# Attention steps that mix side slots, scores and products with v, in place of turns of two steps

## What is computed

```python
x = x + 0.5 * ffn(layernorm(x));  x = x + attention(layernorm(x));  x = x + 0.5 * ffn(layernorm(x))

def ffn(x):            # weights are +1 or -1: 512 -> 1024 -> 1024 -> 256
    h = concatenate([x, -x]);  h = relu(s0 * (h @ k0)) * 2;  h = relu(s1 * (h @ k1)) * 2;  return s2 * (h @ k2)

def attention(x):      # per batch and head, 2048 queries by 2048 keys
    scores = softmax(q @ k.T / 4);  return concat_heads(scores @ v) @ wo.T + bo
```

## Time and profile before

| | us |
|---|---|
| median of 3 runs | 1490.13 |
| lowest and highest run | 1490.06, 1495.2 |
| the profiled execution | 1485.83 |
| its span, first to last instruction | 1481.8 |
| what lies around the span | 4.0 |
| PE busy | 1467.2 |
| ACT busy | 1149.8 |
| DVE busy | 594.7 |

### The profile page before, as it was taken

One profiled execution on the slowest core, in us unless ns is written; L12 is line 12 of the kernel. 1 busy time (PEld: TensorE's weight loads), 2 busy tenths in 40 slices (PEclk: granted clock), 3 DMA queues, 4 the chain that ended last, 5 costly groups with the idle time before them and its releaser, 6 DMA issues.

```text
span 1481.8 us, 69894 instructions
## 1 busy us (share of the span) xinstructions
PE 1467.2 (99%) x32431; PEld 754.9 (51%) x32431; DVE 594.7 (40%) x1330; ACT 1149.8 (78%) x1240; POOL 59.8 (4%) x65
## 2 busy tenths in 40 slices
PE   9999999999999999999999999999999999999999
PEld 4555455544455445545454554564555455445454
DVE  7546755621432253334332332332242342333461
ACT  3221221799999999999999999999899999999821
POOL 2010111001000100010100000000000000000000
PEclk9999999999999999999999999999999999999999
DMA  4121324313221341223222221322212312313010
GB/s 137 49 86 36 92 72 107 95 43 96 74 58 43 102 100 47 72 87 101 90 53 74 81 60 58 89 59 61 84 47 69 86 43 71 87 49 64 25 43 17
DMA packets 113359, 103.93 MB, mean 70 GB/s; under 512 B 58919, under 2 KB 98599, under 8 KB 113063
## 3 DMA queue, kind: packets, MB, share of 16 engines
q1 hardware_dynamic: 112230, 98.61, 25.1%
q10 hardware_dynamic: 832, 0.79, 0.2%
HBM read 61.87 MB, written 25.43 MB: 59 GB/s over the span
## 4 chain that ended last, share of the span: by engine, by line
PE 98%; DVE 1%; DMA 1%; issue 0%; SPq 0%; ACT 0%
PE psum L875 31%; PE psum L916 31%; PE psum L896 14%; PE psum L769 12%; PE psum L781 3%; PE psum L757 3%; PE psum L788 2%; PE psum L801 1%; DMA den_t<-den_rows 0%; DVE den_t L1135 0%; DMA x_sb<-in_x 0%; PE psum L794 0%; DVE stats L1059 0%; DVE xn L1001 0%; SPq L1273 0%
## 5 line engine op out<-in xcount | busy, mean ns | idle before, releaser
L971 ACT ACTIVATE prob<-psum 128x1024 f32<-128x1024 f32 x1024 | 1032.0, 1026 | 64.1 <-PE psum L896 25.6
L916 PE MATMUL psum<-prob,v_sb 64*17 64x512 f32 x8192 | 552.7, 589 | 0.2 <-issue 0.2
L896 PE MATMUL psum<-q_st,k_st 64*32 64x512 f16 (+1 forms) x7736 | 481.3, 376 | 3.2 <-issue 3.1
L944 ACT ACTIVATE h_hi<-psum 128x512 f16<-128x512 f32 x183 | 108.3, 597 | 211.4 <-PE psum L769 165.8
L896 PEld LDWEIGHTS psum<-q_st,k_st 64*32 64x32 f16 (+1 forms) x7736 | 154.1, 92 | 203.2 <-ACT prob L971 77.5
L916 PEld LDWEIGHTS psum<-prob,v_sb 64*17 64x17 f32 x8192 | 152.7, 93 | 147.4 <-issue 80.0
L1011 DVE SCALAR_TENSOR_TENSOR h_lo<-psum,h_hi 128x512 f16<-128x512 f32 x256 | 168.3, 687 | 82.8 <-ACT h_hi L944 80.3
L1009 DVE TENSOR_SCALAR h_hi<-psum 128x512 f16<-128x512 f32 x73 | 50.5, 692 | 369.4 <-PE psum L875 369.4
L875 PE MATMUL psum<-h_lo,w 64*32 64x512 f16 (+1 forms) x4688 | 165.0, 376 | 2.0 <-issue 1.9
L875 PE MATMUL psum<-h_hi,w 64*32 64x512 f16 (+1 forms) x4688 | 164.6, 376 | 0.3 <-ACT h_hi L944 0.2
L875 PEld LDWEIGHTS psum<-h_hi,w 64*32 64x32 f16 (+1 forms) x4688 | 84.7, 93 | 60.6 <-issue 11.0
(11 more groups left out here) (110 smaller groups left out, 878.6 us busy)
## 6 DMA issues: line engine op xcount, KB each, us to landing
k_st<-k_halves SPq DMA_DIRECT2D x256, 128.0 KB, 2.8
q_halves<-piece SPq DMA_DIRECT2D x32, 256.0 KB, 2.5
q_st<-q_halves SPq DMA_DIRECT2D x64, 128.0 KB, 2.6
x_rows<-x_sb SPq DMA_DIRECT2D x16, 256.0 KB, 2.2
k_halves<-piece SPq DMA_DIRECT2D x16, 256.0 KB, 3.0
att_rows<-o_sb SPq DMA_DIRECT2D x128, 32.0 KB
x_sb<-x_rows SPq DMA_DIRECT2D x8, 512.0 KB, 4.5
att_t<-att_rows SPq DMA_DIRECT2D x16, 256.0 KB
```

Source lines behind the costliest of these rows:

```text
L896: mm = pe.matmul(psum[c, SCORES[(h + r) % len(SCORES)], :], k_st[rows, slot, t * P:(t + 1) * P][:, c], q_st[rows, slot, :], start=True, st ...
L916: mm = pe.matmul(psum[32 * j:32 * j + va, O_BANKS[r], :], v_sb[rows, b * key_tiles + t, GROUP * g4 + j, :], prob[rows, h % PROBS, :], star ...
L944: act.activation(hi, psum[:, bank, :], ACT.Relu).then_inc(act_done, 1)
L971: act.activation(prob[:, to:to + 2, :], psum[:, bank:bank + 2, :], ACT.Exp, scale=score_scale / QK_SCALE ** 2).then_inc(exp_sem, 1)
```

## The change

Three things change in the order that is laid, and nothing in what is computed.

1. The loop takes single steps not for l1 alone but for every kind except l3 and v, and except where `sq` follows next but one. The kind is looked at before `lay_turn`, so where a step without slots (such as `merge`) stands at the head of the list, a pair of single steps is taken too, whatever comes behind it.
2. A single step is laid *mixed* (slots, score, values, score, and the same again) where the pair that is under way has more than two gaps left and the step isn't the first of a group's values; else as before. There are 212 single steps now, 105 of them mixed (87 begin in l2, 6 each in l3, qk and out), and 22 turns of two.
3. `lay_turn`, now called for each single step, lays long DVE steps beside l2 only if fewer than 24 slots of the pair are done.

```diff
         if side[0].kind != "l2":
             lay_long(math.inf)
-        else:
+        elif side[0].hi < 24:
             lay_long(1.0)
...
         lay_turn(n)
-        gap = GAP[side[0].kind]
-        for pair in range(2):
-            lay_pair(gap, True)
-            lay_score(4 * n + pair, True)
-        for tile in range(2):
-            lay_values(2 * (n - 1) + tile)
-            lay_score(4 * n + 2 + tile, True)
+        s, gap = side[0], GAP[side[0].kind]
+        if (s.hi if s.n else 0) + 2 * gap < 2 * FILLS[s.kind][0] and n % group_steps != 1:
+            for tile in range(2):
+                lay_pair(gap, True)
+                lay_score(4 * n + 2 * tile, True)
+                lay_values(2 * (n - 1) + tile)
+                lay_score(4 * n + 2 * tile + 1, True)
+        else:
+            for pair in range(2):
+                lay_pair(gap, True)
+                lay_score(4 * n + pair, True)
+            for tile in range(2):
+                lay_values(2 * (n - 1) + tile)
+                lay_score(4 * n + 2 + tile, True)
...
     for n in range(1, att_steps, 2):
-        if side[0].kind == "l1" and n + 1 < att_steps:
+        if side[0].kind not in ("l3", "v") and side[2].kind != "sq" and n + 1 < att_steps:
```

## The result

The changed kernel took a median of 1497.41 us in 16 runs (1490.60 to 1502.12), the kernel before 1490.93 in 16 runs beside it (1485.68 to 1495.51): a ratio of 1.0038 with a 95% interval of [1.0022, 1.0053]. Run again on the chip of the first experiments it was at 1.0010 [0.9987, 1.0033]. Over all its 28 runs its mean is 1495.4 us, that of before over 132 runs 1490.5. So it is slower by some 4.9 us (0.3%; by these means 4.8, give or take 1.6 at 95%). The forecast was 1490, no change.

A forecast was written before the change was run, and what follows sets the result against it. PE was taken to bound attention, 0.05 us over ACT's exp. Terms +4.1 − 2.3 − 1.05 − 0.7 = +0.05 on the profiled 1485.83 us, plus 4.3 for the median, gave 1490.2, rounded 1490; range 1481 to 1498.

The forecast's parts named there:

- The base and the beat: In attention PE sets the beat, 1.077 us a score, 0.05 over ACT's exp; mixing slots and values in l2 costs 0.
- parts 2 to 4: In attention: starts of pairs +4.1 us, swaps of a pair's halves −2.3, l3's switches between narrow and wide −1.05.
- part 5: Pauses where PE lacks instructions in attention: −1.7 us from broken-up slot runs, +1.0 from narrow l3, together −0.7.
- Nine packets at 0.56: In narrow l3 instruction packets last 0.56 us less than today's densest stretch; a fifth of 5 taken, +1.0 us.
- part 4: Twelve of 72 l3 gaps become narrow, three turns without switches: −1.05 us; narrow matmuls take as long as wide ones.
- Two of the three pauses: Two of three PE pauses fell late in long runs of slots, which the change breaks up: −1.7 us.
- parts 2 and 3: Late first slots of pairs, +4.1 us, of which 2.2 behind qk; swaps of halves, −2.3 us, of which −1.4 in qk.
- C: Rival: narrow l3 is paced by its number of matmuls, +10.3 us in 12 gaps, 1499.5 us; chance 0.12.
- D: Rival: narrow l3 starves on instructions, the +5 us of part 5 in full, 1494 us; chance 0.06.
- B: Rival: the even instruction stream ends nearly all pauses in l2, some 9 us, 1481 us; chance 0.24.
- The bound of 0.5%: For the whole kernel, a measurement tells about 0.5% (7.4 us) from no change; no change beyond it had chance 0.64.

The follow-up runs named there:

- e3: The changed kernel with l3 wide again and qk in turns of two steps; 1487.89 and 1488.64 us, 0.9968 and 0.9995 of the kernel before.
- e1: The changed kernel with l3 laid in turns of two steps and wide again; 1490.16 us, 0.9985 of the kernel before.
- e2: The changed kernel with qk in turns of two steps, l3 left as changed; 1492.30 us, 1.0027 of the kernel before.
- e5: The kernel before with all 72 gaps of l3 narrow, in turns of two steps; 1528.52 us, 1.0264 of the kernel before.
- e8: The kernel before with l2 and the scores among its slots wide, as l3 is; 1494.57 us, 1.0037 of the kernel before.
- e9: The kernel before with the second-half fetches of att_t and den_t held back by a turn or more; 1489.71 us, ratio 1.0006.
- e7: As e3, but the second half of each l2 pair in turns of two steps; 1487.54 and 1487.24 us, 0.9983 and 0.9984 of before.
- e4: The changed kernel with every single step unmixed; 1497.06 us, 1.0033 of the kernel before.
- e10: e7 with the second-half fetches of att_t and den_t held back as in e9; 1487.87 us, 0.9978 of the kernel before.

## Why the prediction was wrong

**The base and the beat (right).** PE paces attention and mixed steps of l2 cost nothing by themselves. The changed kernel, PE, two mixed steps:

```profile
938.75 0.41 PE L903 MATMUL psum<-q_st,k_st 64*32 64x512 f16 x8
...
943.05 0.41 PE L903 MATMUL psum<-q_st,k_st 64*32 64x512 f16 x8
...
947.36 0.41 PE L903 MATMUL psum<-q_st,k_st 64*32 64x512 f16 x8
```

8.61 us for eight scores, as in the earlier trace rows. No exp became late for its values.

**Starts, swaps, switches (parts 2 to 4; right in most pieces, the sum in part by luck).** Predicted +4.1 − 2.3 − 1.05 = +0.75; measured +0.4 over all that isn't a pause. But the table's rows of late slots rose by 3.1, where starts, swaps and the switches narrow to wide (3 × 0.14) come to +1.4 (some 0.8 of the rest are late slots of narrow l3), and small excesses elsewhere fell by 2.7, of which the sum had only 0.6. In its pieces: a start of l2 behind l2 costs 0.05 and not 0.03 (the slot at 953.00 stands 0.26 behind its score), one behind qk 0.29 to 0.34 and not 0.28; qk's and out's swaps vanished; a turn of narrow l3 has no switch left. The timeline of that start:

```profile
952.74 0.41 PE L903 MATMUL psum<-q_st,k_st 64*32 64x512 f16 x8
953.00 1.06 PE L882 MATMUL psum<-h_hi,w 64*32 64x512 f16 x32
```

The four swaps of v, which I had not looked at, stayed at 0.16.

**Pauses (part 5; this step failed).** I had found the mechanism, in the earlier trace rows, and had the two effects with their signs. Both were mis-sized. "Nine packets at 0.56 would be 5; most packets come in time, and I take a fifth: +1.0": it was 3.9 us in the profile, and 3.9 to 4.9 net between kernels that differ only in how these three l3 are laid (with 0.8 of late slots and the 1.05 saved by part 4 inside). In three stretches of some nine packets five pauses over 0.38 us appear, so more than half come late, not a fifth, and by 0.5 to 1.1 us each. The right reading was at hand: the pace of use had to be compared with how long a packet takes to come. The trace of the kernel before has it, 0.7 + 1.05 us to its end and some 1.45 more until PE goes on, 3.2 in all: more than 2.8 us each time, and just under the 3.4 us of a run of slots, where a late start shows at once. "Two of the three pauses fell late in such runs: −1.7": breaking up the runs of slots in l2 gave about −2.2 (e3 against before, by means, with its late starts of l2 inside it), a little more. And I had no term for pauses in the slots of v: single steps for qk cost 2.2 to 3.2 us by the means, where parts 2 and 3 have 2.2 − 1.4 = +0.8 for its starts and swaps. In the profiles 1.5, 1.1 and 1.0 us of pauses stand there with qk in single steps (changed twice, e1), none in e2 and e3; the rest isn't placed.

Summed from the runs: −2.2 (single steps in l2 and out), +2.2 to +3.2 (qk), +3.9 to +4.9 (narrow l3): +4.8 in the mean. That it comes to what was measured is no test, since the steps lead from the one kernel to the other; that each of the two effects has the same size within 1.0 us with the other and without it is one.

**The rivals.** C, the pace of the matmuls, is refuted: 0.87 us for 64, in the changed kernel and in e5. The 0.16 us a gap, estimated from the Trainium skill's page "TensorE: Matmul & The Clock Gate", section "Wait — 56ns, not 53.3ns?", don't appear either: the gap is 0.01 over 0.862, so its 2.5 ns are not paid for each of eight tiles in turn. D, narrow l3 starving on instructions, is what happened; it had 0.06, and its +5 was the right price. B had the sign right for l2 and the size wrong: the even stream does lose fewer packets, 2 us and not 9. That both ran against each other is why neither's sum was seen whole.

The Trainium skill, "Runtime: NRT & Kernel Launch", section "Instruction fetch mechanics", has blocks of 256 instructions (16 KiB). The traces agree: stops at a fixed count of 256, 4.29 MB in 262 packets. That crossing costs are mostly hidden, as it says, holds for most packets of the kernel before, and not where narrow matmuls of 256 columns stand (e5: 32 stops inside groups, the kernel before 5).

**The two bases.** I summed against one execution and added 4.3 us for the median without asking what it consisted of. It is, as far as the runs show (e8's spread of 0.6 us, and the clock, below), stops and the clock behind the longest of them: the profiled execution had 11.9 us of pauses, 6.6 of them stops, an average run by the estimate 16.6 and 11.3. A term that scales them had to be sized by the latter. The range, 1481 to 1498, held the median of 1497.41, at its very edge, and the second time (1493.32) the kernel lay well inside. What was wrong is the forecast of no change: the interval of 16 runs each, 1.0022 to 1.0053, leaves it out. The bound of 0.5% for what can be told was too coarse; by it this result would still count as no change, which had 0.64. The ends of the sum, 1479 to 1503, don't follow from the ends of its parts (−12.7 and +10.0 with D, so 1477 and 1500); nothing hangs on them.

**What stays open.** Why a packet starts late in one place or execution and in time in the next: stops recur near 540, 680, 820, 1043 and 1172 us, where transfers are dense, but e9, which took away a part of them, left the stop at 1043. No run took all transfers away from such a place. The third edit (long DVE steps kept from the last quarter of l2) wasn't run alone; nothing in the traces shows an effect.

## What to carry to other kernels

Where PE is the bound and its matmuls are small, count instructions per microsecond over stretches as long as a packet lasts, and not per kernel: what counts is how long the densest run of 256 instructions lasts, beside the time from the end of one block until the next can be used (here some 3.2 us, read from the instruction queue in the trace). A wide matmul laid as four narrow ones took the same time here (0.87 us a gap) and costs four times the instructions; keep such runs short or lay sparser work between them. If a kernel's runs spread by a per cent while every wait in its profile is fixed, look for stops inside groups of like instructions, and compare profiles only after taking these out.

## What the runs showed of the hardware

**A long stop costs again, in the clock.** e7's second profile, by stretches as above:

```profile
1043.40:1046.20 2.80, 0.41 (x13) 1.00 0.48 151
1046.20:1050.00 3.80, 3.78 (x59) 0.55 0.07 21
1050.00:1053.00 3.00, 3.00 (x104) 1.00 0.03 8
```

and in its timeline, PE:

```profile
1046.22 0.39 PE L903 MATMUL psum<-q_st,k_st 64*32 64x512 f16 x3 [2.41 <-issue]
1046.46 1.84 PE L882 MATMUL psum<-h_hi,w 64*32 64x512 f16 x32
1048.03 0.70 PE L903 MATMUL psum<-q_st,k_st 64*32 64x512 f16 x8
1048.45 1.83 PE L923 MATMUL psum<-prob,v_sb 64*17 64x512 f32 x16
1050.09 0.41 PE L903 MATMUL psum<-q_st,k_st 64*32 64x512 f16 x8
```

Behind a stop of 2.8 us the granted clock is at its lower level (1.2 GHz) for some 3.4 us: the gap of slots takes 1.57 us (1046.46 to 1048.03) and not 0.86, the tile 1.64, and the stop costs some 1.7 us more than its own length. In all profiles of the study, within attention, the clock fell behind six of the seven stops of 2.5 us and more, and behind none of 28 between 1.7 and 2.5, the two longest of before (2.26 and 2.24 us) among them. The length alone doesn't decide it: after attention it fell behind a pause of 2.43 us in e4 (1418.4) and didn't behind one of 2.50 in e10 (1414.8). So the profile of before shows none of this cost, but its runs have it: of 116 runs beside the experiments, those with a mean clock of 1.000 took 1487.4 us (31), 0.999 1490.2 (42), 0.998 1492.0 (30), 0.997 1495.0 (11), 0.995 1497.5 (2). These steps hold the stops as well as the clock behind them. The mean clock of e8 was 1.000 in nine of ten runs.

**Small matmuls.** 64 narrow matmuls of 256 columns run in 0.87 us, 13.6 ns apart, as long as instructions are there. The start behind a stop comes 1.2 to 1.7 us behind the end of a packet in nearly all cases. Where PE didn't stop, a packet started 0.7 us behind the end of the block before and lasted 1.05 us (medians). The spread of the kernel's time (a standard deviation of 3.2 us over 132 runs) falls to 0.6 us with a quarter of l2's instructions (e8), and was 7.1 us with dense l3 (e5, four runs).
